# Attention heads: VectorE divides a head's sums of values ahead of its first marking of the round

## The reference, cut to what matters

```
_, draft_indices = jax.lax.top_k(draft, num_remain)   # 128 keys for each query
mask = mask.at[b_idx, h_idx, s_idx, draft_indices].set(0.0)
mask = jnp.where(causal_future[None, None, :, :], neg, mask)
scores = jnp.einsum('bhqd,bhkd->bhqk', qr, kr) / np.sqrt(HD) + mask
attn = jax.nn.softmax(scores, axis=-1)
out = jnp.einsum('bhqk,bhkd->bhqd', attn, v)
```

## Time and profile before

| what | value |
| --- | --- |
| median of 3 runs | 3397.38 us (3397.19 to 3402.8) |
| the profiled execution | 3398.37 us, its span 3396.6 us |
| mean granted clock of TensorE | 0.907 |
| busy: TensorE, VectorE, ScalarE, GpSimd | 3019.7, 2404.0, 1961.9, 1532.1 us |

### The profile page before, as it was taken

How to read it: one execution, slowest core, us unless ns; L and a number is a source line. 1 busy time by engine, 2 the same in 40 slices (tenths; PEclk the granted TensorE clock), 3 DMA queues, 4 the chain that set the end, 5 groups by cost and what they waited for, 6 DMA issues and landing times. The chain is left out here.

```text
span 3396.6 us, 49801 instructions
## 1 busy us (share of the span) xinstructions
PE 3019.7 (89%) x15644; PEld 1834.0 (54%) x15737; DVE 2404.0 (71%) x4659; ACT 1961.9 (58%) x4170; POOL 1532.1 (45%) x3508
## 2 busy tenths in 40 slices
PE   7999999999999999999999877487888788888779
PEld 4455454554554645545445435266666666666654
DVE  5677696786876967769679428587777777777640
ACT  1464564545545635456455115788888888888621
POOL 2245263362442633625426200766666666666410
PEclk9999999999999999999999988577777777777889
DMA  2222132231322322313212010000000000000010
GB/s 83 62 84 84 70 116 81 69 106 68 97 72 79 115 74 81 91 71 106 87 53 97 13 45 1 1 1 1 1 2 1 2 2 1 1 2 1 1 48 25
DMA packets 65800, 169.58 MB, mean 50 GB/s; under 512 B 11776, under 2 KB 19328, under 8 KB 64512
## 3 DMA queue, kind: packets, MB, share of 16 engines
q1 hardware_dynamic: 54448, 115.17, 10.5%
q10 hardware_dynamic: 11088, 51.19, 4.3%
HBM read 161.08 MB, written 5.24 MB: 49 GB/s over the span
## 5 line engine op out<-in xcount | busy, mean ns | idle before, releaser
L1898 ACT ACTIVATE X<-ah_z,ah_trial 128x256 bf16<-128x256 f32 (+6 forms) x896 | 732.4, 824 | 25.0 <-POOL ah_trial L2001 13.9
L1082 ACT ACTIVATE m_mix<-m_mix,m_cs 128x128 f32<-128x128 f32 x1024 | 312.9, 388 | 257.2 <-DMA m_mix<-cs_rows 257.2
L1853 PE MATMUL ah_ps_o<-a_v,X 128*128 128x17 f32 x2304 | 353.3, 282 | 44.8 <-DVE hT L2098 44.8
L1853 PEld LDWEIGHTS ah_ps_o<-a_v,X 128*128 128x128 f32 x2304 | 337.9, 220 | 52.1 <-ACT X L1909 49.7
L1909 ACT ACTIVATE X<-ah_ps_e 128x512 f32<-128x512 f32 (+3 forms) x384 | 185.8, 485 | 191.5 <-PE ah_ps_e L1840 128.5
L2070 DVE TENSOR_SCALAR_CACHE_REDUCE X<-ah_z,ah_cut 128x256 bf16<-128x256 f32 (+6 forms) x224 | 193.6, 875 | 128.7 <-POOL ah_cut L2006 128.7
L964 POOL TENSOR_TENSOR m_xdec<-m_xdt,m_decay_out 128x512 f32<-128x512 f32 x112 | 142.8, 1275 | 213.1 <-DVE m_xdt L1208 202.0
L887 PE MATMUL m_ps_x<-m_w_out,m_gate 128*128 128x512 f32 x512 | 234.1, 600 | 0.0
L887 PE MATMUL m_ps_d<-m_w_out,m_gate 128*128 128x512 f32 x512 | 233.5, 599 | 0.0
L2083 DVE MAX8 ah_top<-ah_ps_m 128x8 f32<-128x256 f32 (+6 forms) x224 | 185.9, 830 | 67.0 <-PE ah_ps_m L1803 58.8
L992 POOL TENSOR_TENSOR m_squares<-m_squares 128x256 f32<-128x256 f32 x128 | 104.1, 813 | 276.9 <-ACT m_squares L1094 276.9
(11 more groups left out here) (297 smaller groups left out, 7518.9 us busy)
## 6 DMA issues: line engine op xcount, KB each, us to landing
m_mix<-cs_rows SPq DMA_DIRECT2D x128, 512.0 KB, 4.5
m_w_proj<-in_w_proj ACTq DMA_DIRECT2D x69, 512.0 KB, 3.3
m_fade<-fade_rows SPq DMA_DIRECT2D x224, 128.0 KB, 3.0
m_w_out<-in_w_out ACTq DMA_DIRECT2D x7, 2048.0 KB, 7.7
X<-in_x SPq DMA_DIRECT2D x8, 256.0 KB, 5.0
m_w_out<-in_w_out SPq DMA_DIRECT2D x1, 2048.0 KB, 10.6
x_away<-X SPq DMA_DIRECT2D x1, 2048.0 KB, 10.9
X<-x_away SPq DMA_DIRECT2D x8, 256.0 KB, 7.3
```

Of the source, the lines that this page charges most:

```text
L1082: act.activation(mix[:, u % 3, h, :], mix[:, u % 3, h, :], ACT.Relu, bias=cs[:, c, h0 + h:h0 + h + 1], scale=-1.0).then_inc(lag_done, 1)
L1853: last = pe.matmul(ps_o[:, t, :], eT[:, g % 3, b * P:(b + 1) * P], v[:, b0 + b, h // REP, :], start=i == 0 and b == 0, stop=b0 + b == t, s ...
L1898: act.activation(sign[:, at % 2, 0:(t + 1) * P], z[:, h % RING, cols(t)], ACT.Sign, bias=trial[:, h % RING, 0, t - 1:t], scale=-1.0, accum ...
```

## The change

The call of `divide(n - 4)` stands ahead of `take(n - 2, 1)`, where it stood behind `take(n - 2, 3)`. Nothing else is changed: instructions, shapes, tiles and semaphores are the same.

```diff
                     sample(n + 1)
                     evacuate(n + 1, 0)
                     add_sample(n + 1)
+                if live(n - 4):
+                    divide(n - 4)
                 if live(n - 2):
                     take(n - 2, 1)
                     take(n - 2, 2)
...
                         evacuate(n + 1, t)
                     if live(n - 2) and t + 2 < NT:
                         take(n - 2, t + 2)
-                    if t == 1 and live(n - 4):
-                        divide(n - 4)
```

## The result

The changed kernel takes 3344.53 us (median of 4 runs, 3341.27 to 3345.71), the kernel before 3397.28 us (4 runs, 3392.56 to 3402.8): a ratio of 0.9846, with a 95% interval of 0.9834 to 0.9858. The forecast was 3345 us.

A forecast was written before the change was run, and what follows sets the result against it. No engine is full; a chain through several, with TensorE's wait for the division on it, bounds the round. 3398.4 - 44.8 - 8 = 3345.6 us, taken as 3345 us for a median; range 3320 to 3380 us.

The forecast's parts named there:

- The old place: At a head's first product, TensorE's 31 waits for the division, 1.45 us each, go and pass on fully: -44.8 us.
- The new place: Ahead of the first marking, the division's 0.45 us hides in VectorE's wait for the cut: 0, at most 12 us.
- GpSimd beside it: The division running while GpSimd computes the cut does not hold GpSimd up: 0, at most +12 us.
- The clock: TensorE's granted clock over the full rounds gains from less idle time: -8 us, bounds 31 us to either side.
- The clock paying in full: Rival: the lower clock ends earlier in each round, each gaining 1.15 us more: 3322 us, 15%.
- The second rival: Tile 2 starts earlier but at the lower clock for longer, losing part of the gain: 3363 or 3384 us, 16%.
- VectorE would be held in front of the marking: Rival: the old head's last product comes late, so the division delays the marking: 3411 us, 5%.

The follow-up runs named there:

- the two filled kernels: The kernel before and that with the division ahead of the third marking, useless matmuls added ahead of marked scores of tiles 4 and 5: 3371.47 and 3351.8 us.
- the kernel with the division half of the way up: The kernel before with the division one instruction earlier, ahead of the third marking instead of behind it: 3394.95 us, ratio 1.0003.
- The filled second place: The changed kernel with three useless matmuls ahead of the marked scores of tile 4 and eight ahead of tile 5's: 3293.27 us, ratio 0.9696.
- the filled first place: Six useless matmuls ahead of the marked scores of tile 1, in the changed kernel and in the kernel before: 3346.69 and 3395.11 us.
- the filled one half of the way up: The kernel before with the division ahead of the third marking and useless matmuls ahead of marked scores of tiles 4 and 5: 3351.8 us, ratio 0.9868.
- the kernel with the division two instructions up: The kernel before with the division behind the pick of tile 1, ahead of the evacuation and third marking: 3375.53 us, ratio 0.9931.

## Why the prediction was right, point by point

**What bounds the kernel.** Right. TensorE's wait for the division lies on the chain that bounds the round: the changed kernel with the wait kept by another condition is back at 3395.89 us, and the one with VectorE's time kept stays at 3341.56.

**The old place, -44.8 us.** The wait did go: 44.8 to 0.2 us. That it passes on one for one was the step's claim. It came out so between the two filled kernels (19.7 us for 20.1 us of wait), and fails in the kernel as it is: the first 20 us of the wait are worth nothing, the rest everything. It fails inside the changed kernel too. Over the 24 rounds 35.9 us of waiting for the division went, but TensorE's wait for the first marking grew from 39.4 to 50.7 us, so that a good part of the removed wait stands elsewhere. The sum came out because the whole wait was taken away and because the clock gave more than its term; that the forecast lies within 0.5 us of the result is luck. Had I been asked for the kernel with the division half of the way up, the same reasoning would have said 3374 us, as its expectation did, and the chip said 3394.95.

**The new place, 0 us.** Right, and shown: without the division 3344.64 us, with it 3344.53. I had 0.13 us to spare in the tightest round; the round shown above has 1.2. There the old head's last eight products took 1.02 us, where the earlier trace rows has 1.81: they ran before the clock fell.

**GpSimd beside it, 0 us.** Right by the same run. The Trainium skill's condition (SBUF — State Buffer, Who interferes with whom), two inputs in SBUF, is not met by a division that reads PSUM, and the result, no cost, agrees with that.

**The clock, -8 us.** Right in sign, too small in size, and for a reason that was misread. The mean over 24 rounds rose from 0.77 to 0.79, and TensorE's busy time in the 27 full rounds fell by 17.9 us, where the term had 8. Their length fell by 45.7 us, so TensorE's idle time fell by 27.8, where 27 x 1.45 = 39 of waiting for the division were gone. The rest of the 53.8 us lies in the rounds before and behind them and after the last cut, where four of the 31 waits stood too. The terms of 44.8 and 8 us are thus not what was measured, only their sum is. The prediction put the lower stretch right behind the two idle places. The row 2810.10:2812.70 above shows it begun 2.8 us ahead of the cut, ahead of both. The prediction gave the clock a bound of 31 us; the filled kernels show 34 us with the second part of the wait.

**The rivals.** The clock paying in full (3322 us) did not come by the change, but was there to be had: 3293.27 us by filling one idle place. The Trainium skill (TensorE: Matmul & The Clock Gate, What's actually happening) says that activity releases the throttle. The filled second place agrees with that (0.79 to 0.94), and the filled first place does not show it (0.77 and 0.77). The second rival, part of the gain lost on the way, did not come by the change; it came true half of the way up, with all of it lost. That VectorE would be held in front of the marking did not occur: the division left 1.2 and 0.78 us there.

**What stays open.** Why the rounds of kernels with quite different waits have the same mean length was not settled: 34.09 to 34.14 us with waits of 44.8, 31.1 and 24.9 us and with 29 us of idle time filled, and 32.42 and 32.43 us for the changed kernel and the filled one half of the way up. The lengths in between (33.41 and 33.24 us) say that it is a pull and no law. The traces show what goes with it: rounds and clock run in step. With the division half of the way up, the lower stretch lies from 1.7 us ahead of the cut to 8.5 behind it, in the round with the cut at 2533.52 and again thirteen rounds later, at 2977.21:

```profile
2531.80:2542.00 10.20, 6.87 (x40) 5.28 (x42) 6.67 (x25) 8.23 (x22) 9.12 (x32) 0.50 0.00 1
2975.50:2985.70 10.20, 6.87 (x40) 5.25 (x42) 6.62 (x25) 8.24 (x22) 9.12 (x32) 0.50 0.00 1
```

Which of the two sets the pace no run shows. Nor is it settled why filling the second idle place works and the first does not: the clock is still up ahead of the second, and mostly down at the first, but where the filling did move the fall at the first, nothing was gained either. A kernel with two accumulators for the sums of values, in which TensorE would not have to wait for the division, wasn't tried.

## What to carry to other kernels

A wait that is removed by half may give nothing, and the other half may give double: where the granted clock changes within a loop's round, measure the whole step before giving up on a half one. Read the round's length beside its mean clock, and sum the busy and idle time over many rounds: a wait that shrinks while the length stays has gone into the clock or into another wait. Where TensorE waits in the middle of a round for another engine and the clock falls there, a few useless matmuls in that place can be worth as much as the reordering: here 51 us on top of the change's 53. A sum that comes out shows its total and not its terms.

## What the runs showed of the hardware

- A full round took 34.1, 32.4 or 30.7 us on average for groups of kernels whose waits for the division differ by up to 25 us in all, with 24-round means equal within 0.07 us. Two kernels lay in between, at 33.4 and 33.2. I had expected every tenth of a microsecond of wait to show.
- TensorE's clock fell to its lower level in the rounds of both kernels (means of 0.75 to 0.82), although their idle places are 0.4 to 2.3 us long. Eleven matmuls of 256 columns in the place of 1.45 us and its neighbour raised the mean clock from 0.79 to 0.94; six in the place of about 2 us changed it in neither kernel by more than 0.01.
- One execution of the kernel with the division two instructions up had a clock of 0.54 and 0.50 over 67 us behind the last cut, and was 22 us slower than the median of its five runs.
